# The order of shared and routed work, and the place of fetches and a root, in a two-stage mixture-of-experts kernel with attention between

## What is computed

```python
scores = sigmoid(x2d @ router_weight.T)           # 16 experts in 4 groups
# two groups kept, four experts per token, weights normalised, times 2.5
h = silu(g) * u                                   # per expert, inner width 128
routed = einsum('te,teh->th', combine, yo)
shared = _mlp(x)                                  # inner width 256
x = x + 0.5 * (routed + shared)
x = x + attention(layernorm(x))                   # conv, scan, gate, norm, projection
x = x + 0.5 * ffn(layernorm(x))
```

## Time and profile before

| | us |
|---|---|
| median of three runs | 1458.34 (1457.24 to 1463.23) |
| the profiled execution, span from first to last instruction | 1457.1 |
| TensorE busy | 1277.6 |
| GpSimd busy | 971.7 |
| VectorE busy | 893.7 |
| ScalarE busy | 626.6 |
| median landing of a fetch of a quad (512 KB) | 4.1 |
| median landing of a store of y (256 KB) | 2.9 |

### The profile page before, as it was taken

The page is one execution under the profiler, slowest core; times in us unless marked ns, Lnnn a source line. Parts: engine busy times, 40 slices in busy tenths (PEclk is TensorE's granted clock), DMA queues, the critical chain, the costliest instruction groups (busy, mean ns, idle before and its releaser), DMA issues.

```text
span 1457.1 us, 23386 instructions
## 1 busy us (share of the span) xinstructions
PE 1277.6 (88%) x6904; PEld 1101.4 (76%) x6904; DVE 893.7 (61%) x2190; ACT 626.6 (43%) x1088; POOL 971.7 (67%) x1340
## 2 busy tenths in 40 slices
PE   5697999999967699999999999996988399999990
PEld 5595888888855578888888887785877388888870
DVE  5765722354628997877878787767657322354553
ACT  2153344444315456566566565561342134434420
POOL 3588880584848597787978879531757870384876
PEclk9898999999988899999999999997989799999995
DMA  9974585687743201000000000214434464587753
GB/s 353 410 276 170 167 305 180 213 281 234 240 160 134 91 2 44 16 30 16 30 30 29 29 0 30 81 30 167 176 134 168 134 241 167 196 263 251 233 173 113
DMA packets 86919, 218.43 MB, mean 150 GB/s; under 512 B 16272, under 2 KB 28560, under 8 KB 85904
## 3 DMA queue, kind: packets, MB, share of 16 engines
q1 hardware_dynamic: 62224, 149.82, 28.8%
q0 software_dynamic: 24576, 67.14, 14.6%
HBM read 109.43 MB, written 107.48 MB: 149 GB/s over the span
## 4 chain that ended last, share of the span: by engine, by line
PE 50%; DVE 17%; POOL 14%; issue 12%; ACT 3%; DMA 3%; POOLq 0%; DVEq 0%; SPq 0%; ACTq 0%; another core or an unknown queue 0%
PE ps L1082 10%; POOL f_gbuf L493 8%; PE ps L1116 8%; PE ps L1087 6%; PE ps L1050 4%; DVE at_xs L1854 4%; PE ps L2054 4%; PE ps L2056 4%; PE ps L2055 4%; PE ps L2115 3%; POOL xg L467 2%; PE ps L1066 2%; PE ps L2104 1%; PE ps L2116 1%; DMA f_gbuf<-yg,f_rows 1%
## 5 line engine op out<-in xcount | busy, mean ns | idle before, releaser
L493 POOL DMA_INDIRECT f_gbuf<-yg,f_rows x256 | 268.4, 1048 | 214.9 <-DMA yg<-f_yo 155.1
L467 POOL DMA_INDIRECT xg<-f_xn,f_rows x256 | 251.8, 984 | 113.6 <-DVE f_rows L770 59.7
L1082 PE MATMUL ps<-f_wgu,f_xT 128*128 x1248 | 297.4, 381 | 3.1 <-DVE f_hT L823 3.1
L1082 PEld LDWEIGHTS ps<-f_wgu,f_xT 128*128 128x128 f32 x1248 | 226.4, 191 | 28.0 <-issue 3.3
L819 DVE TENSOR_TENSOR f_h<-ps,f_sg 128x256 f32<-128x256 f32 x156 | 66.0, 423 | 248.5 <-ACT f_sg L547 247.7
L1116 PE MATMUL ps<-f_wd,f_hT 128*128 x624 | 163.7, 385 | 39.7 <-ACT f_yo L556 20.7
L547 ACT ACTIVATE f_sg<-ps 128x256 f32<-128x256 f32 x156 | 59.9, 384 | 313.6 <-PE ps L1082 313.6
L843 DVE SCALAR_TENSOR_TENSOR f_xin<-f_gbuf,f_w,f_xin 128x256 f32<-128x256 f32 x256 | 125.4, 490 | 75.4 <-DMA f_gbuf<-yg,f_rows 68.3
L1116 PEld LDWEIGHTS ps<-f_wd,f_hT 128*128 128x128 f32 x624 | 117.9, 192 | 61.0 <-issue 45.4
L1087 PE MATMUL ps<-f_xT,f_wgu_sh 128*128 128x256 f32 x512 | 132.5, 413 | 23.7 <-DVE f_hT L823 23.7
L1854 DVE SCALAR_TENSOR_TENSOR at_xs<-at_raw,at_taps,at_xs 128x512 f32<-128x512 f32 x136 | 140.2, 1033 | 8.1 <-POOL at_xs L1505 3.9
(11 more groups left out here) (258 smaller groups left out, 2708.3 us busy)
## 6 DMA issues: line engine op xcount, KB each, us to landing
f_xq<-xg SPq DMA_DIRECT2D x78, 512.0 KB, 4.1
yg<-f_yo SPq DMA_DIRECT2D x156, 256.0 KB, 2.9
xg<-f_gbuf SPq DMA_DIRECT2D x39, 512.0 KB, 17.8
f_wgu<-in_gate_up SPq DMA_DIRECT2D x4, 1280.0 KB, 15.3
f_xin<-in_x SPq DMA_DIRECT2D x8, 512.0 KB, 7.0
xg<-f_xn,f_rows POOLq DMA_INDIRECT x256
f_gbuf<-yg,f_rows POOLq DMA_INDIRECT x256, 3.8
x<-f_xin SPq DMA_DIRECT2D x8, 512.0 KB, 4.0
```

The lines of the kernel that those rows point to most:

```text
L467: G.indirect_dma_start(xg[0:USED[g] * P, :], bass.IndirectOffsetOnAxis(ap=rows[g][:, b, k:k + 1], axis=0), xn[:, SUB * TILE0[g] + b, :], N ...
L493: G.indirect_dma_start(gbuf[:, n % GBUF, k, :], None, yg[0:USED[g] * P, :], bass.IndirectOffsetOnAxis(ap=rows[g][:, b, k:k + 1], axis=0), ...
L1082: last = T.matmul(gu_ps[:, j % 2, s * 2 * P:(s + 1) * 2 * P], x_of(k, s, d), weight(wgu[:, :, d, :], experts[s]), start=(d == 0), stop=(d ...
```

## The change

In the first stage the routed pairs of group 0 start after shared pair 4: shared pairs 5 and 10 move behind group 0's routed pairs, and pair 11 moves behind all routed pairs, ahead of 12 to 15. So the first routed pair is at slot 24 and not 30, and group 1's at 44 and not 46. VectorE's routing pieces move with their events: weights of group 1 (`order_weights`) to the first two routed pairs, group 2's pieces one routed pair later, counts and names likewise. Three combines of group 2 instead of two stand inside the shared pairs (`FINAL`). Since pair 11's part may now be added after the combine of the same tokens, `take_part` and `combine` wait for whichever of the two comes first in their order, and a tile's store waits for both.

GpSimd in the first stage runs attention's root after block 8 of group 1's fetch, not after the whole fetch.

In both stages SP's fetches have a new place. Quads 8 to 11 come behind the store of y11 (they came behind y2, y4, y6 and y8 in both stages). Every other quad comes behind the first store whose slot is at or past the slot before the one that frees its buffer. In both stages quads 13, 14 and 15 now come behind y16; from quad 16 on the place relative to the slots is as before. In the second stage nothing else changes.

```diff
 def ffn_events(fresh):
-    for r in range(0, 6):
-        yield "route", r
-    for r in range(0, 2 if fresh else 4):
-        yield "shared", r
...
+    yield from each("route", 0, 1, 2, 3, 4, 5)
     if fresh:
+        yield from each("shared", 0, 1)
+        yield from each("both", 6, 7, 8, 9)
+        yield from each("route", 10, 11)
+        yield from each("shared", 2, 3)
+        yield from each("route", 12, 13, 14, 15)
+        yield from each("shared", 4)
     else:
+        yield from each("shared", 0, 1, 2, 3)
+        yield from each("both", 6, 7, 8, 9)
+        yield from each("route", 10, 11)
+        yield from each("shared", 4)
+        yield from each("route", 12, 13, 14, 15)
+        yield from each("shared", 5)
     for g in range(NG):
         for i in range(RP[g]):
             yield "routed", (g, i)
-        if g == 0 and not fresh:
-            for r in (10, 11):
-                yield "shared", r
-    for r in (12, 13, 14, 15):
-        yield "shared", r
+        if g == 0:
+            yield from each("shared", *((5, 10) if fresh else (10, 11)))
+    if fresh:
+        yield from each("shared", 11)
+    yield from each("shared", 12, 13, 14, 15)
...
+    def stored_from(self, s):
+        return min(n for n in range(sum(RP)) if self.of_pair(n) + DOWN_ROUTED >= s)
...
-    FINAL = [("shared", 14), ("shared", 15)]
+    FINAL = [("shared", r) for r in ((13, 14, 15) if fresh else (14, 15))]
...
+    LATE = 2 if fresh else 1
+    COUNT_AT = [("shared", 0) if fresh else ("route", 5), ("route", 15), ("routed", (0, 4 + LATE))]
+    PACK_AT = [("both", 6) if fresh else ("shared", 3), ("routed", (0, 1)), ("routed", (0, 10 + LATE))]
...
         def store_tile(t):
             sp.wait_ge(combined, SUB * (t + 1))
+            sp.wait_ge(part_out, max(part_of(2 * t), part_of(2 * t + 1)))
...
+        def loaded_behind(q):
+            if 2 * q >= RP[0] and q < RP[0] // 2 + XQ:
+                return RP[0] - YO - 1
+            return SLOTS.stored_from(SLOTS.turned_in(at_event["routed", routed_pair(2 * (q - XQ) + 1)]) - 1)
...
-            if n % 2 == 0 and XQ + early + n // 2 < pairs // 2:
-                load_quad(XQ + early + n // 2)
+            for q in range(XQ + early, pairs // 2):
+                if loaded_behind(q) == n:
+                    load_quad(q)
...
-                if g == NG - 1 and b in (2, 3, 4):
+                if (g, b) in ((1, 8), (2, 2), (2, 3), (2, 4)):
                     next(other, None)
...
-        gather_group(0)
-        gather_group(1)
-        next(other, None)
-        gather_group(2)
+        for g in range(NG):
+            gather_group(g)
...
+            before = [n for n in added if n // 2 == r]
+            if before:
+                dve.wait_ge(combined, before[-1] + 1)
...
-            if (kind, n) == ("shared", 5):
+            if (kind, n) == ("routed", (0, 0)):
                 route_piece(1, 8)
-            if (kind, n) == ("shared", 10):
+            if (kind, n) == ("routed", (0, 1)):
                 route_piece(1, 9)
...
-            if kind == "routed" and n[0] == 0 and n[1] > 0:
-                route_piece(2, n[1] - 1)
+            if kind == "routed" and n[0] == 0 and n[1] >= LATE:
+                route_piece(2, n[1] - LATE)
```

More of the change, by code:

```diff
@@ L94, in ffn_events, with each @@
 def ffn_events(fresh):
-    for r in range(0, 6):
-        yield "route", r
-    for r in range(0, 2 if fresh else 4):
-        yield "shared", r
[L100 to L103, removed]
-    if fresh:
-        for r in range(2, 4):
-            yield "shared", r
-    else:
[L108 to L114, removed]
-        for r in (10, 11):
-            yield "shared", r
+    def each(kind, *pairs):
+        for r in pairs:
+            yield kind, r
+    yield from each("route", 0, 1, 2, 3, 4, 5)
+    if fresh:
+        yield from each("shared", 0, 1)
[4 more added lines that the diff above has]
+        yield from each("shared", 4)
+    else:
+        yield from each("shared", 0, 1, 2, 3)
[4 more added lines that the diff above has]
+        yield from each("shared", 5)
     for g in range(NG):
@@ L334, in ffn_stage @@
     FILL = [0] + [n // 4 for n in USED]
-    FINAL = [("shared", 14), ("shared", 15)]
+    FINAL = [("shared", r) for r in ((13, 14, 15) if fresh else (14, 15))]
     ROUTES = [(k, n) for k, (kind, n) in enumerate(EVENTS) if kind in ("route", "both")]
-    COUNT_AT = [("shared", 0) if fresh else ("route", 5), ("route", 15), ("routed", (0, 5))]
-    PACK_AT = [("both", 6) if fresh else ("shared", 3), ("shared", 5) if fresh else ("routed", (0, 1)), ("routed", (0, 11))]
+    LATE = 2 if fresh else 1
+    COUNT_AT = [("shared", 0) if fresh else ("route", 5), ("route", 15), ("routed", (0, 4 + LATE))]
+    PACK_AT = [("both", 6) if fresh else ("shared", 3), ("routed", (0, 1)), ("routed", (0, 10 + LATE))]
     shifted = DIRECT if fresh else 0
@@ L352, in outputs_before, with part_of @@
         return sum(kind in kinds for kind, _ in OUTPUTS[0:yy])
+    def part_of(r):
+        return outputs_before(("both", "shared"), [m for _, m in OUTPUTS].index(r)) + 1
     SLOTS = Slots(EVENTS)
@@ L827, in take_hT @@
             V.tensor_copy(hT[:, j % 4], hT_bank[SLOTS.routed_before(j) % 2][:, 0:2 * P]).then_inc(hT_copied, 1)
+        added, parts = [], []
         def take_part(s, yy):
@@ L831, in take_part @@
             r = OUTPUTS[yy][1]
+            before = [n for n in added if n // 2 == r]
+            if before:
+                dve.wait_ge(combined, before[-1] + 1)
+            parts.append(r)
             part = xin[:, r // 2, 2 * (r % 2):2 * (r % 2) + 2, :].rearrange("p s d -> p (s d)")
@@ L839, in combine @@
             new_chain()
-            dve.wait_ge(part_out, outputs_before(("both", "shared"), [m for _, m in OUTPUTS].index(r)) + 1)
+            if r in parts:
+                dve.wait_ge(part_out, part_of(r))
+            added.append(n)
             dve.wait_ge(gathered[n % GBUF], 64 * (nth * NB // GBUF + n // GBUF + 1))
```

## The result

The changed kernel takes 1437.6 us (median of four runs, 1433.6 to 1440.1), the kernel before 1459.0 beside it: ratio 0.9847, interval 0.9823 to 0.9870. It is 21.4 us faster where 25.6 were expected, so 4.2 of the gain are missing; the total is 4.9 above the forecast of 1432.7, because the kernel before was itself 0.7 slower here than in the forecast's own runs.

The account below looks back on a forecast made before the run. It took TensorE, held by a blocked quad 8 fetch, to bound the second stage, and VectorE from 440 to 540 us to bound the first stage's end. 1458.34 - 19.4 - 6.2 = 1432.7 us, range 1424 to 1446.

Parts of the forecast that it names:

- Term 1: Second stage: quad 8 fetched behind y11 lets slot 44's matmuls start 20.4 us earlier, less 1.0 for the clock: -19.4 us.
- Rival (c): Second stage's gain does not reach the end because GpSimd's scatters and fetches set it: 1450 to 1458 us, chance 0.07.
- Term 2: First stage's end: in_proj and VectorE's saturated stretch 4.2 us earlier, plus 2.0 for one combine fewer: -6.2 us.
- The start: First stage: longer waits for quad 0 and attention's flag make routed pairs of group 1 and later run 4 us later.
- The 1.8 us of blocked stores: First stage: ScalarE's wait on blocked stores, counted among the standing of 16.7 us now and nothing after.
- The root: First stage's end: attention's root runs at about 400.5, inside the second fetch, so VectorE's 12.3 us wait for it goes.
- its bound of -10.2: First stage's end: the largest gain allowed, reached with 0 us of lateness at the start because the flag wait does not grow.
- In_proj: First stage's end: in_proj goes out at 425.0 against 429.23, and VectorE's saturated stretch starts 4.2 us earlier with it.
- The combine: First stage's end: group 2's first combine runs at shared 13 while VectorE waits for in_proj, saving 2.0 us.
- rival (a): Only the second stage pays; the first gives 0 or loses a little: 1438 to 1446 us, chance 0.20.
- Rival (b): The first stage pays in full, TensorE not late at its start: 1424 to 1428 us, chance 0.12.
- Rival (d): Slower than before: TensorE's low clock lasts through group 0's sixteen routed pairs after the start's idle times: 1484 us, chance 0.03.

Follow-up runs that it names:

- e1: Kernel before with only the second stage's new fetch places (quads 8 to 11 behind y11, the rest by the new rule): 1442.3 us, ratio 0.9883.
- e2: Kernel before with only attention's root moved inside the second fetch, after its block 8: 1450.0 us, ratio 0.9937.
- e3: Kernel before with the second stage's new fetch places and the root inside the second fetch, old first-stage order: 1431.0 us, ratio 0.9810.
- e9: e3 with in_proj, out_proj and x's second tile loaded ahead of tile 5's store: 1427.9 us, ratio 0.9773.
- e7: Changed kernel with in_proj, out_proj and x's second tile loaded ahead of tile 5's store: ratio 0.9842.
- e12: Changed kernel with two combines of group 2 inside the shared pairs instead of three, the one at shared pair 13 back behind in_proj's split: ratio 0.9876.
- e8: e3 with in_proj loaded ahead of tile 5's store and, in the first stage, quads 8 to 11 behind y9: ratio 0.9829.
- e11: e10 with in_proj, out_proj and x's second tile loaded ahead of tile 5's store: ratio 0.9774.
- e4: Changed kernel with root and both stages' fetches back at their old places, leaving only the new first-stage order: 1477.3 us, ratio 1.0118.
- e5: Changed kernel with shared pair 5 back ahead of the routed pairs: ratio 0.9833.
- e6: Changed kernel with VectorE's naming and weights of group 1 one event later, at the first routed pair: ratio 0.9863.
- e10: e5 with quads 8 to 11 behind y9 instead of y11 in the first stage: 1426.2 us, ratio 0.9774.

## Why the prediction was right, and where its sizes were off

**Term 1 (-19.4) is right, by its own steps.** Quad 8 is issued at 1159.6 as forecast; the matmuls of slot 44 start at 1163.9 (1163.4 was worked out); the clock costs 1.65 (1.0 taken, 1.7 the bound). The stage is 20.1 shorter in the changed kernel and 19.4 in e1. By the runs of e1 the term is 17 to 18, so it may be 1 or 2 short. From the issue of the four fetches to quad 8's turn it was 3.9 us (4.7 in e1), and not the 8.5 of the last of four in the earlier trace rows, which an equal share would have taken. The Trainium skill ("DMA: Bandwidth & Descriptors", "Two DMAs through the same engine are not ordered") has descriptors in one queue of one DMA engine start in order, and this fits it. The other figure that the prediction took from that page ("Anatomy of one DMA") is given there for DMAs that GpSimd issues, while these fetches are SP's; nothing in the sum rests on it. The term's lower bound was added up wrongly: 20.4 less 5.1 for the landing and 1.7 for the clock is 13.6, not 14.6, which would have put the range's joined bound at 1445.5. Rival (c) is out with this term: GpSimd still waits 40.9 us for stores at a stretch, 59.0 before.

**Term 2 (-6.2) is where, by the traces, the missing gain is.** There it is -1.7: attention ends so much earlier. By the runs it is 3 to 5, which is what the changed kernel has over e1 (medians 3.2, ratios 0.0036), with intervals that overlap; so a miss in this term is shown, and its size only to some 3 us. Four of its steps, in order:

*The start: "4 us later" was 5.5.* The waits were right almost to the tenth: 14.76 and 6.93 us, 14.5 and 6.9 forecast; so was the clock, 7.0 x 0.35 = 2.5 and 5.6 x 0.42 = 2.4 for 3.0 and 2.5. The 1.8 us of blocked stores were not TensorE's: ScalarE's wait goes, but TensorE's own idle time there, 1.6 us for VectorE in the kernel before, is 1.8 after. Without that credit the sum of the forecast is 6.4 instead of 4.6, which I then rounded down to 4. The 5.5 is from two traces, but holds up: the second fetch starts between 347.6 and 349.1 in the five kernels with the old order and the old fetches of the first stage (before, e1, e2, e3, e9), and between 353.1 and 354.3 in the changed kernel, e7 and e12.

*The root: right in kind, and worth more.* With the start not moved the forecast's terms give 8.2 at in_proj and 2.0 for the combine, its bound of -10.2. e2, which has no combine to move, gives 10.6 at in_proj and -10.3 at the end of attention. So the root alone is worth 2.4 more than the forecast gave it; 1.3 of that can be the gate and the part of pair 11, which the forecast had ahead of tile 5's store and e2 does not have there.

*In_proj: "4.2 earlier" was 3.1 at the issue and 0.6 at the split.* This step failed. I moved the split with the issue. But the third fetch, which I had moved ahead of it myself (422 in the forecast's own words, aligned 424.0), goes with a load that lands late: ScalarE could start 8.7 us after the issue, and 6.5 before. In the fourteen kernels this falls into two sets without overlap. Where in_proj is issued ahead of the third fetch or within 0.1 us of it (before, e1, e2, e3, e7, e8, e9, e11) it takes 6.0 to 6.7 us to ScalarE's cast; where it is issued 2.1 behind the start of that fetch (changed, e4, e5, e6, e10, e12), 8.7 to 9.5. The fetch pays in either order: VectorE's combine starts 7.5 us after the fourth and last gather of its block is issued (430.78 to 438.24), and 6.5 in e7 and 6.6 in e11, where in_proj goes first; a gather lands in 3.8 by the median. So the first block of the third fetch was not in by 431, as the forecast had it, but at 435.4 aligned. Over the 12 us from the issue of in_proj the DMA engines had no share left, 1.01 busy at 377 GB/s in the kernel before and 0.98 at 349 GB/s in the changed one, and the two commands of in_proj landed after 8.2 us by their median before and 11.1 after. That load and gathers slow each other in transfer is what this says; the order of their packets was not looked at.

*The combine: right, as far as two traces tell.* The 2.0 it was to save are 1.8 by e12. But it is also a second lock on the split: with the loads ahead (e7, e11) it alone holds VectorE. Moving in_proj on top of the combine pays nothing; without the combine (e9) it paid some 2 us, inside the noise.

So the two sides of the first stage nearly cancel: root and combine give some 12 (10.3 and 1.8), and the order takes 10 of it back: 5.5 at the start, 2.0 more by the issue of in_proj (3.1 earlier where 10.6 less 5.5 are left), 2.2 in its landing. That the total came as near to the forecast as it did is in part luck: the root was worth up to 2.4 more than the forecast gave it, and that set off a part of what the start and the issue and landing of in_proj took beyond it. **The mechanism was that of the forecast, the size of term 2 is rival (a)'s**, which had the first stage give nothing and 1438 to 1446; the measured 1437.6 lies between the two. Rival (b) needed TensorE not to be late. Rival (d) is out: behind both waits the clock was back at 1.00 (2.4 GHz) by 144 us. The prediction's ground for that named 21 us of idle time too, which the earlier trace rows does not show; the trace has it, a clock of 0.64 over the 5.0 us behind TensorE's 20.66.

What the prediction could not show is what e3, e4 and e10 do: the order is a cost of 17 us by itself, of some 5 beside the other two edits, and none that the runs can tell when shared pair 5 stays ahead of the routed pairs and the fetches come behind y9. The routed pairs must not reach quad 0 earlier than VectorE and GpSimd can have it; each 5.6 us pair that leaves that place buys only idle time there.

e9 and e3 differ by 5 us by their ratios, but by some 2 in the traces and by 1.6 when each median is laid beside that of the kernel before in its own rounds (31.2 and 29.5 us faster), so 2 is the likelier size. What stays open is why the second stage is 429 us in e7 and e11 and 432 to 435 in most others with the same code there.

## What to carry to other kernels

Look in an in-order queue for a command that waits for something far off and sits ahead of commands that are ready; moving it back to its own deadline gave 17 to 20 us here, and that deadline is counted in slots, so it has to be set again whenever the order of the work changes (in the first stage y11 in slot 39 served for a turn in slot 42; in slot 41 it did not, and y9 in slot 43 did not for a turn in slot 44: three slots were enough, and one slot cost 4.7 and 5.2 us). When work is pulled ahead, ask first whether its input is there: the work that leaves was the cover of that wait. And when a load and a large gather are moved towards each other, do not carry over the landing time that either had alone.

## What the runs showed of the hardware that was not expected

From the issue of in_proj to its use were 6.0 to 6.7 us in eight kernels and 8.7 to 9.5 in six, and the two sets differ in whether it was issued ahead of GpSimd's fetch (or with it) or 2.1 us into it. The later place is the dearer one, though the DMA engines are full in both (1.01 in the kernel before, 0.98 in the changed one, over 12 us).

The same idle time is not followed by the same clock. After 3.32 us of standing for the flag the kernel before had 0.70 over the next 5.6 us, and so had e1, e2, e6, e8 and e9; e3 had 0.50, e5 and e10 the full clock. e10 and e11 have the same work up to there, the same wait of 10.8 us ahead of it and the flag at 132.16 and 132.15, and differ only in loads that come 280 us later. First e10, then e11:

```profile
132.10:140.00 7.90, 7.84 (x42) 6.71 (x43) 3.01 (x9) 4.77 (x10) 6.52 (x11) 1.00 0.36 108
...
132.10:140.00 7.90, 7.85 (x34) 6.73 (x34) 1.48 (x5) 3.91 (x8) 6.53 (x11) 0.78 0.36 125
```

So the wait and the work ahead of it do not settle the clock behind it, and what a forecast can say of a wait of this length here is 0 to 3.2 us (e5 and e10 at 1.00; e3 with 0.60 over 7.9 us). What makes the difference no run here tells.
